# GpSimd leaves the recurrence of a four-layer graph network on one core

## The reference, cut to what matters

```
for _ in range(5):
    m  = adj @ h
    u3 = h @ u3_w.T + u3_b
    z  = sigmoid(m2 @ w3_w.T + w3_b + u3)          # m2 = concat(m, m)
    r  = sigmoid(m2 @ w4_w.T + w4_b + u3)
    v  = tanh(m2 @ w5_w.T + w5_b + (r * h) @ u5_w.T + u5_b)
    h  = (1 - z) * h + z * v
```

## Time and profile before

| | us |
|---|---|
| median of three runs | 2041.39 |
| profiled execution | 2039.13 |
| its span | 2036.8 |
| PE busy | 1856.7 (91%) |
| DVE busy | 1472.1 (72%) |
| ACT busy | 1354.7 (67%) |
| POOL busy | 921.1 (45%) |

### The profile page before, as it was taken

The page is one execution under the profiler, slowest core; times in us unless marked ns, Lnnn a source line. Parts: engine busy times, 40 slices in busy tenths (PEclk is TensorE's granted clock), DMA queues, the critical chain, the costliest instruction groups (busy, mean ns, idle before and its releaser), DMA issues.

```text
span 2036.8 us, 27531 instructions
## 1 busy us (share of the span) xinstructions
PE 1856.7 (91%) x9307; PEld 1442.9 (71%) x9307; DVE 1472.1 (72%) x3054; ACT 1354.7 (67%) x2689; POOL 921.1 (45%) x1009
## 2 busy tenths in 40 slices
PE   3899998899998999889998899989999889989997
PEld 2776776777767777577775777757768677676775
DVE  6786688766687667866778667786667866678666
ACT  0766677576766767566775667756768666686666
POOL 2354445445364442634436344363444544345344
PEclk6999999999999999999999999999999999999998
DMA  2000001000010000100000000100001000000000
GB/s 69 22 1 0 1 1 42 1 1 1 7 37 1 1 1 12 32 1 0 1 24 21 1 1 1 43 1 1 1 2 42 0 1 1 2 22 1 0 1 22
DMA packets 13514, 21.32 MB, mean 10 GB/s; under 512 B 2720, under 2 KB 5024, under 8 KB 13216
## 3 DMA queue, kind: packets, MB, share of 16 engines
q1 hardware_dynamic: 10768, 18.68, 2.7%
...
...
## 4 chain that ended last, share of the span: by engine, by line
PE 65%; DVE 13%; issue 8%; POOL 7%; ACT 7%; DMA 0%; DVEq 0%; SPq 0%; POOLq 0%; ACTq 0%
PE psA L1080 7%; PE psA L1050 7%; PE psA L1051 7%; PE psA L881 5%; PE psB L886 5%; PE psB L888 5%; PE psB L887 5%; PE psA L886 3%; PE psA L888 3%; PE psA L887 3%; PE psB L949 3%; PE psA L949 3%; DVE E L753 2%; ACT X L471 2%; PE psB L1074 2%
## 5 line engine op out<-in xcount | busy, mean ns | idle before, releaser
L430 POOL TENSOR_TENSOR S<-S,H 128x512 f32<-128x512 f32 x160 | 225.1, 1407 | 486.3 <-ACT S L573 486.3
L1050 PE MATMUL psA<-adjT_hi,nh_hi 128*128 128x512 f32 x640 | 275.0, 430 | 11.9 <-ACT H L559 11.6
L471 ACT ACTIVATE X<-X,shift,rstd 128x128 f32<-128x128 f32 x512 | 210.4, 501 | 90.2 <-POOL shift L401 89.2
L1051 PE MATMUL psA<-adjT_hi,nh_lo 128*128 128x512 f32 x640 | 259.8, 406 | 0.0
L425 POOL TENSOR_TENSOR xT_lo<-H,xT_hi 128x512 fp32r<-128x512 f32 x160 | 219.2, 1383 | 71.0 <-ACT xT_hi L581 38.1
L841 DVE SCALAR_TENSOR_TENSOR E<-E 128x512 f32<-128x512 f32 x160 | 181.7, 1135 | 63.3 <-ACT E L577 60.4
L836 DVE SCALAR_TENSOR_TENSOR E<-E,H 128x512 f32<-128x512 f32 x160 | 128.5, 803 | 115.1 <-ACT E L567 114.7
L679 DVE TENSOR_TENSOR gT_lo<-psA,gT_hi 128x512 fp32r<-128x512 f32 x160 | 108.8, 688 | 115.0 <-ACT gT_hi L563 101.1
L396 POOL TENSOR_TENSOR neg_mean<-zero_cols,mv 128x4 f32<-128x4 f32 x128 | 30.8, 240 | 356.1 <-DVE mv L696 355.8
L1080 PE MATMUL psA<-E,u5T 128*128 128x512 f32 x320 | 165.0, 597 | 13.7 <-DVE E L836 13.7
L571 ACT ACTIVATE E<-psB,z_bias 128x512 f32<-128x512 f32 x160 | 110.4, 690 | 81.3 <-PE psB L1074 79.8
...
## 6 DMA issues: line engine op xcount, KB each, us to landing
...
```

The lines of the kernel that those rows point to most:

```text
L430: nc.gpsimd.tensor_tensor(kept[s], kept[s], H[s][:, :], ALU.mult).then_inc(pool_done[s], 1)
L471: last = nc.scalar.activation(X[s][:, t, :], X[s][:, t, :], ACT.Identity, scale=rstd[s][:, t:t + 1], bias=shift[s][:, t:t + 1])
L1050: nc.tensor.matmul(psA[s][:, :], hi, adjT_hi[:, m, :], start=(m == 0), stop=False)
L1051: last = nc.tensor.matmul(psA[s][:, :], lo, adjT_hi[:, m, :], start=False, stop=(exact and m == TILES - 1))
```

## The change

The lower part of the state moves from GpSimd to a new stage uh of the vector engine. The update h = h + z(v - h) is three operations of the vector engine: v - H, (z+1) times that, and H + 0.5 of that; ScalarE's copy, GpSimd's product and the semaphores keep_done go. GpSimd has no stage in the recurrence any more. The orders of all four engines are written out as lists in place of SCHEDULE and `body`'s arithmetic, and they differ from the old ones in many places. TensorE has the same stages as before. The core of the diff, with the stretches of the lists that are spoken of below:

```diff
+ORDER = {
+    "tensor": (
+        "x0.1 x0.0 -v4.3 -rh4.3 -t4.2 query.0 x0.2 -t4.3 query.1 x0.3 scores01.0 query.2 scores01.1 scores23.0 "
...
+        "scores01.2 query.3 scores23.1 mix.0 scores23.2 scores01.3 mix.1 scores23.3 mix.2 x1.0 mix.3 x1.1 xh.0 xh.1 "
+        "x1.2 gates.0 x1.3 edges.0 gates.1 edges.1 xh.2 agg.0 gates.2 xh.3 sums1.0 edges.2 agg.1 gates.3 self.0 "
...
+        "rh0.1 v0.2 t0.0 rh0.2 v0.3 rh0.3 t0.1 m1.0 t0.2 m1.1 t0.3 m1.2 uh1.0 r1.0 m1.3 v1.0 uh1.1 uh1.2 r1.1 r1.2 "
...
+        "uh2.2 r2.0 uh2.3 v2.0 r2.2 rh2.0 r2.3 v2.1 rh2.1 v2.2 t2.0 rh2.2 v2.3 rh2.3 t2.1 m3.0 t2.2 m3.1 t2.3 m3.2 "
...
+        "uh4.0 m4.1 r4.0 t3.2 t3.3 v4.0 rh4.0 uh4.1 r4.1 m4.2 v4.1 t4.0 rh4.1 uh4.2 r4.2 m4.3 v4.2 rh4.2 t4.1 uh4.3 "
+        "r4.3 "
+    ),
...
+    "vector": (
+        "-r4.2 -spread3.0 -m4.3 -last.1 -rh4.2 -r4.3 -spread3.1 x0.0 -last.2 -rh4.3 x0.1 -spread3.2 -last.3 query.0 "
...
+        "spread0.0 scores01.3 scores23.2 sums0.1 scores23.3 spread0.1 sums0.2 x1.0 spread0.2 sums0.3 x1.1 spread0.3 "
+        "xh.0 xh.1 gates.0 edges.0 x1.2 x1.3 gates.1 xh.2 edges.1 gates.2 xh.3 sums1.0 edges.2 gates.3 self.0 sums1.1 "
...
+        "lap_lo.1 lap1.3 lap_lo.3 lap2.1 spread2.0 lap2.3 spread2.1 x3.0 uh0.0 spread2.2 spread2.3 x3.1 uh0.1 m0.0 "
...
+        "m2.1 t1.3 uh2.3 m2.0 uh2.2 m2.2 m2.3 r2.0 r2.2 r2.1 rh2.0 r2.3 rh2.1 t2.0 rh2.2 uh3.0 t2.1 rh2.3 t2.2 uh3.1 "
...
+        "t3.3 uh4.1 m4.1 t3.2 rh4.0 uh4.2 r4.1 m4.2 last.0 uh4.3 rh4.1 "
+    ),
+    "gpsimd": (
+        "-spread3.0 -spread3.1 -spread3.2 spread0.0 -spread3.3 spread0.1 spread0.2 spread0.3 x1.2 x1.0 x1.3 x1.1 "
...
+    out = []
+    for token in ORDER.get(engine, "").split():
+        name, slot = token.lstrip("-").split(".")
+        out.append((name, int(slot), int(token.startswith("-"))))
+    return out
...
-            def stage_m(s, r, k):
-
-                pool.wait_ge(xT_hi_ready[s], XT_HIS * r + XT_HI["x3" if k == 0 else f"h{k - 1}"])
-                if k == 0:
-                    pool.wait_ge(copied[s], COPIES * r + COPIED["x3"])
-                nc.gpsimd.tensor_tensor(xT_lo[s][:, :], H[s][:, :], xT_hi[s][:, :].bitcast(F32), ALU.subtract).then_inc(pool_done[s], 1)
-
-            def stage_v(s, r, k):
-
-                pool.wait_ge(keep_done[s], STEPS * r + k + 1)
-                nc.gpsimd.tensor_tensor(kept[s], kept[s], H[s][:, :], ALU.mult).then_inc(pool_done[s], 1)
...
-                act.wait_ge(z_done[s], STEPS * r + k + 1)
-                nc.scalar.activation(kept[s], z_gate[s], ACT.Copy, scale=-0.5, bias=0.5).then_inc(keep_done[s], 1)
...
+            def stage_uh(s, r, k):
+                dve.wait_ge(xT_hi_ready[s], XT_HIS * r + XT_HI["x3" if k == 0 else f"h{k - 1}"])
+                if k == 0:
+                    dve.wait_ge(copied[s], COPIES * r + COPIED["x3"])
+                lo_part(xT_lo[s][:, :], H[s][:, :], xT_hi[s][:, :]).then_inc(vector_done[s], 1)
...
                 dve.wait_ge(hv_done[s], STEPS * r + k + 1)
+                nc.vector.tensor_tensor(h_new[s], h_new[s], H[s][:, :], ALU.subtract).then_inc(vector_done[s], 1)
+                dve.wait_ge(vector_done[s], VECTORS * r + VECTOR[f"diff{k}"])
+                dve.wait_ge(z_done[s], STEPS * r + k + 1)
                 nc.vector.scalar_tensor_tensor(out=h_new[s], in0=z_gate[s], scalar=1.0, in1=h_new[s],
                                                op0=ALU.add, op1=ALU.mult).then_inc(vector_done[s], 1)
                 dve.wait_ge(vector_done[s], VECTORS * r + VECTOR[f"update{k}"])
-                dve.wait_ge(pool_done[s], POOLS * r + POOL[f"kept{k}"])
-                nc.vector.scalar_tensor_tensor(out=H[s][:, :], in0=h_new[s], scalar=0.5, in1=kept[s],
+                nc.vector.scalar_tensor_tensor(out=H[s][:, :], in0=h_new[s], scalar=0.5, in1=H[s][:, :],
                                                op0=ALU.mult, op1=ALU.add).then_inc(vector_done[s], 1)
...
-                pe.wait_ge(pool_done[s], POOLS * r + POOL[f"h_lo{k}"])
+                pe.wait_ge(vector_done[s], VECTORS * r + VECTOR[f"h_lo{k}"])
```

More of the change, by code:

```diff
@@ L35 @@
 EPS = 1e-5
[L41 to L116, removed]
-def body(engine):
[L122 to L134, removed]
+ORDER = {
+    "tensor": (
[12 rows of a table added]
+    ),
+    "scalar": (
[12 rows of a table added]
+    ),
+    "vector": (
[12 rows of a table added]
+    ),
+    "gpsimd": (
[3 rows of a table added]
+    ),
+}
@@ L156 @@
     ["rsum", "elu_low1", "elu1", "src_bias", "self", "elu_low2", "elu2"]
-    + [f"{name}{k}" for k in range(STEPS) for name in ("rh", "update", "h")])}
+    + [f"{name}{k}" for k in range(STEPS) for name in ("h_lo", "rh", "diff", "update", "h")])}
 POOL = {name: n + 1 for n, name in enumerate(
@@ L160 @@
      "neg_mean1", "var1", "rstd1", "shift1", "bias2", "neg_mean2", "var2", "rstd2", "shift2"]
-    + [f"{name}{k}" for k in range(STEPS) for name in ("h_lo", "kept")] + ["neg_mean3", "var3", "rstd3", "shift3"])}
+    + ["neg_mean3", "var3", "rstd3", "shift3"])}
 TURNS, XTS, GTS, NHS, COPIES, PRODUCTS, VECTORS, POOLS = map(len, (TURNED, XT, GT, NH, COPIED, PRODUCT, VECTOR, POOL))
@@ L272, in build @@
         rh = [E[s][:, 3, :] for s in range(SLOTS)]
-        kept = [S[s][:, 1, :] for s in range(SLOTS)]
         s_adj, s_qk, s_gru, s_cheb, s_small = sem("s_adj"), sem("s_qk"), sem("s_gru"), sem("s_cheb"), sem("s_small")
@@ L297, in build @@
         r_done, z_done, hv_done = sems("r_done"), sems("z_done"), sems("hv_done")
-        keep_done = sems("keep_done")
         xT_lo_ready, gT_lo_ready, nh_lo_ready = sems("xT_lo_ready"), sems("gT_lo_ready"), sems("nh_lo_ready")
@@ L435, in _ @@
                 stages[f"spread{n}"] = lambda s, r, n=n: norm(s, r, n)
-            for k in range(STEPS):
-                stages[f"m{k}"] = lambda s, r, k=k: stage_m(s, r, k)
-                stages[f"v{k}"] = lambda s, r, k=k: stage_v(s, r, k)
             run("gpsimd", stages, 0, first=True)
@@ L866, in _ @@
                 stages[f"m{k}"] = lambda s, r, k=k: stage_m(s, r, k)
+                stages[f"uh{k}"] = lambda s, r, k=k: stage_uh(s, r, k)
                 stages[f"r{k}"] = lambda s, r, k=k: stage_r(s, r, k)
```

## The result

The changed kernel takes 2060.51 us (median of 4 runs, 2058.18 to 2060.9); the kernel before, run beside it, 2040.65 (2039.12 to 2041.62). The ratio is 1.0096, 95% interval 1.008 to 1.0112: 1% slower, where 0.7% faster was forecast.

What follows compares the result with a forecast made beforehand. The prediction took TensorE to set the pace in the recurrence, with time to gain only at the borders: 7.8 + 3.2 + 5.6 + 1 - 3 = 14.6 us off 2039.1, said as 2025; 8-in-10 range 1998 to 2052.

Steps and rivals of the forecast that it cites:

- Loads and durations: Vector engine: subtractions at 0.69 us, L841, L845 and L836 back to 690 ns, net 1572 us busy; ScalarE falls by 10.
- Step borders: Between recurrence steps, m3.2 comes 0.1 to 0.2 us late on the vector engine; 32 x 0.1 = 3 us lost.
- The second rival: At borders of two recurrence steps the vector engine's queue delays TensorE: 42 us against the gains, 2063 us; chance 0.20.
- The loop's end: At the loop's jump, rh4.2 starts earlier on TensorE; 1.3 us gained six times, 7.8 us, bounds 0 and 13.
- Layer 0 to layer 1: x1.0's lower part ahead of spread0.2 lets xh.0 follow x1.1 directly; 8 x 0.7 = 5.6 us gained, bounds -10 and 13.
- The start of the recurrence: TensorE's 0.40 us wait for GpSimd's late lower part goes, eight times; 3.2 us gained, bounds -4 and 7.
- the bound of -4: Lower bound for the start of the recurrence: spread2.1, now behind lap2.3, is late by 0.5 us.
- Behind the loop: After the loop, ScalarE's new list can start the norms at once; 1 us gained, bounds 0 to 3.
- The third rival: Shorter gaps save 40% of the time lost to TensorE's lowered clock: 24 us more, 2001 us; chance 0.12.

Runs made afterwards that it cites:

- e3: The changed kernel with m4.3 moved ahead of spread3.0 in the vector engine's list at the loop's start; 2043.76 us, ratio 1.0026 to the kernel before.
- e17: The changed kernel with five places of the vector engine's list in layer 1 put back as in the kernel before; 2069.68 us, ratio 1.0156.
- e6: The changed kernel with e3's exchange, layer 1's stages in the old order on all engines, and spread2.1 ahead of lap2.3 on the vector engine; 2031.96 us, ratio 0.9962.
- e16: New arithmetic in the kernel before's lists, step 0's lower parts right behind x3, slot 2's r and slot 3's m of step 4 ahead of the jump; 2024.43 us, 0.9936.

## Why the prediction was wrong, point by point

- **Loads and durations: right.** 0.69 us for a subtraction, none of the three recurrence operations stretched any more, the vector engine at 1545 us (1572 forecast), ScalarE down by 9 in 100 us (10 forecast). The forecast saw that this is worth nothing where TensorE is full.
- **Step borders, 3 us: right in kind.** PE 100 of 100 us, round 0's recurrence 0.2 us longer with the start's 0.4 in it. The second rival (42 us) gives the right sign and nearly the right time, 2063, by a mechanism that did not happen.
- **The loop's end, gain of 7.8: this is the step that failed, and by the most.** "spread3.0 stands ahead of m4.3 now [...]; it comes just in time". It does come just in time for the matmul: r4.3 at 1040.07 shows no wait. But TensorE's way through the jump starts at that wait, 4.1 us before x0. I had read the 1.68 us of the earlier trace rows as a fixed cost that stays, and the sum has no term for it. It is what is left of 3.9 us from rh4.2's wait (1028.78 - 1024.88), the other 2.2 being covered by queued matmuls; a later last wait lays more of it bare, 17.7 us over the six passes against 10.2 before and 9.5 in e3, and the clock falls behind it. e3 measures the token at 17 us, 14 without round 0's share; with it mended the step would have been a gain, 874.2 + 329.2 - 867.6 - 325.0 = 10.8 by the table.
- **Layer 0 to layer 1, gain of 5.6: wrong in sum.** xh.0 comes right behind x1.1 (1085.64 and 1086.04), and the exchange is worth at least its price (e17). But I followed two slots and stopped. The layer as a whole lost 7.5 us: its idle time grew by only 1.8, and TensorE stood at 1.2 GHz for 30.7 us in it in place of 17.1. The sum had no term for the clock there. Which of the moved tokens brings it on stays open.
- **The start of the recurrence, gain of 3.2: wrong sign, +5.6.** GpSimd's late lower part is gone, as forecast. The case named for the bound of -4 came true, and 5.6 lies beyond it: I had written that spread2.1's "result was lying ready before", and behind lap2.3 it no longer is (e6 gives 4.4 of the 5.6 back there).
- **Behind the loop, gain of 1: nothing came.** From the last round's first product to the end 136.8 us before and 136.6 after.
- **Clock.** The third rival asked whether shorter gaps bring it back. In e3, with less idle time around the jump, layer 0 keeps 1.00 behind all six; in after it falls behind five, at 1.6 us each. So the mechanism is there, but the gap before x0 alone does not tell when: with 1.68 us before, the clock was at 0.50.
- **Was the arithmetic worth it?** With both places moved ahead of the jump, new arithmetic and mended lists take 0.9911 (0.9897 to 0.9924) of the time before, old arithmetic and old lists 0.9915 (0.9902 to 0.9928). No difference can be told. Both beat the two kernels of this case; what they share is two operations ahead of the jump. With the same move, the new arithmetic in the old lists stays a little behind, at 0.9936 (e16).
